# Cross attention and a mixture of experts in one kernel: output projection over pairs of heads, and ten subtractions per batch moved to GpSimd

## The reference

```python
# attention: B=8 batches, N=512 tokens, M=1024 keys, 8 heads of 64, D=256
q, k, v = layernorm(x) @ Wq, context @ Wk, context @ Wv
attn = softmax(q @ k.T * 64 ** -0.5)          # by head
x = x + tanh(g_xattn) * (concat_heads(attn @ v) @ Wo + bo)
# experts: 4096 tokens, 8 experts, the best 2 of each token, capacity 1280
h = layernorm(x)
top2, selected = top_k(softmax(h @ router.T), 2)
y = (pre(h) * silu(gate(h))) @ post           # by expert, DFF=1024
x = x + tanh(g_ffn) * scatter_add(y * weight)
```

## Time and profile before

| | |
|---|---|
| time, median of 3 runs | 1711.11 us (1710.55 to 1712.54) |
| profiled execution, its own time | 1709.52 us |
| its span | 1707.8 us |
| attention, to the first expert matmul | about 1079 us |
| a middle batch, start to start | 131.4 us |
| TensorE, VectorE, ScalarE, GpSimd busy | 96%, 74%, 61%, 39% of the span |

### The profile page before, as it was taken

The page is one execution under the profiler, slowest core; times in us unless marked ns, Lnnn a source line. Parts: engine busy times, 40 slices in busy tenths (PEclk is TensorE's granted clock), DMA queues, the critical chain, the costliest instruction groups (busy, mean ns, idle before and its releaser), DMA issues.

```text
span 1707.8 us, 33525 instructions
## 1 busy us (share of the span) xinstructions
PE 1640.7 (96%) x12454; PEld 1494.2 (87%) x12454; DVE 1262.5 (74%) x2597; ACT 1048.9 (61%) x2179; POOL 672.5 (39%) x629
## 2 busy tenths in 40 slices
PE   6999999999999999999999998989999999999997
PEld 5788888888888888888888886889999999999997
DVE  6888888888888888888888878666565656547443
ACT  5767766666766767667766667536454555546443
POOL 3352444444345345345245334423343422332322
PEclk9999999999999999999999999999999999999999
DMA  4300210111121121031031032314423421341211
GB/s 127 125 26 1 93 71 26 76 75 39 56 96 38 36 106 48 15 124 51 13 125 39 14 137 72 134 42 110 115 39 108 113 37 29 109 115 29 38 33 27
DMA packets 60555, 115.49 MB, mean 68 GB/s; under 512 B 6616, under 2 KB 48480, under 8 KB 59776
## 3 DMA queue, kind: packets, MB, share of 16 engines
q1 hardware_dynamic: 37104, 79.24, 13.1%
q0 software_dynamic: 15392, 18.66, 6.1%
q10 hardware_dynamic: 7920, 15.73, 2.6%
HBM read 90.27 MB, written 57.42 MB: 86 GB/s over the span
## 4 chain that ended last, share of the span: by engine, by line
PE 73%; DVE 13%; issue 5%; POOL 4%; ACT 3%; DMA 2%; POOLq 0%; ACTq 0%; DVEq 0%; SPq 0%; another core or an unknown queue 0%
PE ring L1236 11%; PE turned L1130 10%; PE ffn L1093 10%; PE ffn L1095 10%; PE ffn L1094 10%; PE scores L1118 9%; DVE neg_max L1931 5%; PE ring L1093 3%; PE ring L1095 3%; PE ring L1094 3%; DVE pt_l L1708 3%; PE ring L1202 1%; DMA out<-y,y_token 1%; PE ring L1204 1%; POOL lists L884 1%
## 5 line engine op out<-in xcount | busy, mean ns | idle before, releaser
L918 POOL TENSOR_SCALAR probs<-probs,row_rec 128x1024 f32<-128x1024 f32 x254 | 282.3, 1124 | 465.9 <-DVE row_rec L2035 454.4
L1472 ACT ACTIVATE pt_h<-turned 128x512 fp32r<-128x512 f32 x512 | 278.7, 601 | 208.1 <-PE turned L1130 208.1
L1708 DVE TENSOR_TENSOR pt_l<-turned,pt_h 128x512 fp32r<-128x512 f32 x512 | 331.6, 680 | 6.4 <-ACT pt_h L1472 6.4
L1931 DVE TENSOR_REDUCE neg_max<-scores 128x1 f32<-128x1024 f32 x256 | 302.3, 1217 | 34.7 <-PE scores L1118 34.6
L1130 PE MATMUL turned<-ident,probs 128*128 128x128 f32 x2048 | 281.1, 279 | 27.0 <-DVE pt_l L1708 19.6
L1130 PEld LDWEIGHTS turned<-ident,probs 128*128 128x128 f32 x2048 | 223.9, 141 | 94.9 <-issue 61.6
L1528 ACT ACTIVATE probs<-scores,neg_max 128x1024 f32<-128x1024 f32 x256 | 285.3, 1116 | 13.8 <-DVE neg_max L1931 12.6
L1236 PE MATMUL ring<-pt_h,v_hl 128*128 128x256 f32 x1024 | 261.3, 293 | 0.8
L1236 PE MATMUL ring<-pt_l,v_hl 128*128 128x256 f32 x1024 | 250.7, 283 | 0.0
L2301 DVE TENSOR_TENSOR act_f<-ffn,silu 128x256 f32<-128x256 f32 (+1 forms) x232 | 108.4, 467 | 125.7 <-ACT silu L1642 114.8
L1236 PEld LDWEIGHTS ring<-pt_h,v_hl 128*128 128x128 f32 x1024 | 195.7, 191 | 4.9 <-issue 3.6
(11 more groups left out here) (260 smaller groups left out, 3903.0 us busy)
## 6 DMA issues: line engine op xcount, KB each, us to landing
lists<-pads SPq DMA_DIRECT2D x8, 4160.0 KB
w_raw<-w_t ACTq DMA_DIRECT2D x10, 1024.0 KB, 8.7
e_rows<-lists SPq DMA_DIRECT2D x26, 390.0 KB
ctx_raw<-ctx_t SPq DMA_DIRECT2D x15, 512.0 KB, 3.8
wg_raw<-wg_t ACTq DMA_DIRECT2D x5, 1024.0 KB, 7.7
x_in<-x SPq DMA_DIRECT2D x8, 512.0 KB, 4.1
x_sum<-x SPq DMA_DIRECT2D x8, 512.0 KB, 3.9
out<-x_sum SPq DMA_DIRECT2D x8, 512.0 KB, 2.9
```

Source lines behind the costliest of these rows:

```text
L918: nc.gpsimd.tensor_scalar(probs[:, k, :], probs[:, k, :], row_rec[:, k:k + 1], 1.0, ALU.mult, ALU.mult).then_inc(scaled, 1)
L1472: return nc.scalar.activation(dst, src, ACT.Copy)
L1708: return nc.vector.tensor_tensor(dst, src, hi_part.bitcast(F32), ALU.subtract)
L1931: nc.vector.tensor_reduce(neg_max[:, k:k + 1], scores[:, n % 2, :].rearrange("p (a c) -> p a c", a=2), AX.XY, ALU.max, negate=True).then_i ...
```

## The change

The values of two heads now lie so that one head's own rows are 0 to 63 and the other's 64 to 127: the two heads fill one tile of 128 rows, `ot_h` by pairs. The rows with the product of v's low halves go to `o_low` by ScalarE, VectorE writes `o_rest` (value minus its high half), and GpSimd adds both to `ot_l` (`join_low`, one for two `o` jobs, at each step divisible by 4). A `w` job is two pairs by three passes: 6 matmuls, and it waits for GpSimd's join (`ot_done`). Wo is held once, and is split in one piece. VectorE's subtraction after an `o` job waits for ScalarE's first copy alone; TensorE waits for both copies.

Ten of the 16 k and v jobs of a batch (`POOL_LOWS`) are no longer drained by VectorE: ScalarE copies the bank a second time, raw, into `raw_of_job`, and that releases the bank; GpSimd subtracts later, at the steps of `POOL_LOWS_AT`. The first batch keeps these on VectorE, the last has eight of them.

```diff
@@ FIRST_JOBS
-    15: [("w", 0, 0)],
-    16: [("w", 0, 1), ("k", 3, 0)],
-    17: [("v", 1, 3)],
+    16: [("w", 0, 0), ("k", 3, 0)],
+    17: [("v", 1, 3), ("w", 0, 1)],
     18: [("h", 1, 0)],
-    19: [("w", 0, 2), ("l", 0, 0)],
-    20: [("k", 3, 1), ("q", 3, 0)],
+    19: [("l", 0, 0)],
+    20: [("w", 0, 2), ("k", 3, 1), ("q", 3, 0)],
@@
+POOL_LOWS = [("k", 1, 0), ("k", 1, 1), ("k", 2, 0), ("k", 2, 1), ("v", 1, 0), ("v", 1, 1), ("v", 1, 2),
+             ("v", 1, 3), ("v", 0, 0), ("k", 0, 0)]
+POOL_LOWS_AT = {2: [0], 4: [1], 10: [2], 12: [3, 4], 16: [5, 6], 18: [7], 26: [8, 9]}
@@ gpsimd
+            def join_low(body, u):
+
+                i = ((u - 6) // 4 * 2 + 1) % (2 * H)
+                part, m = i // 4 % 2, i // 2 % 2
+                toks = slice(m * 2 * P, (m + 1) * 2 * P)
+                o = ("o", i, 0)
+                wait_drained(pool, body, body.where[o] if u > 0 else body.before.where[o] - RING)
+                pool.wait_ge(low_copied, at(body.b - 1 if u < 5 else body.b, 2 * H, i + 1))
+                alone(pool)
+                nc.gpsimd.tensor_tensor(ot_l[:, part, toks], o_rest[:, part, toks], o_low[:, part, toks],
+                                        ALU.add).then_inc(ot_done, 1)
+
+            def low_of_job(body, n):
+
+                kind, i, j = POOL_LOWS[n]
+                wait_drained(pool, body, body.where[POOL_LOWS[n]])
+                raw = raw_of_job[:, RAW_SLOT[n], :]
...
+                nc.gpsimd.tensor_tensor(dst, raw, hi_part.bitcast(F32), ALU.subtract)\
+                    .then_inc(lows_split, 1)
@@ gpsimd step, behind the scaling of the probabilities
+                    if u == 0 and body.prev or u % 4 == 0 and body is not END and \
+                            (body.prev if u < 8 else body.own):
+                        join_low(body, u - 2)
+                    if body.prev and body.own:
+                        for n in POOL_LOWS_AT.get(u, ()):
+                            if POOL_LOWS[n] in body.where:
+                                low_of_job(body, n)
@@ tensor
-                    o = ("o", H * i + H // 2 + 1 + j // 2 * 2, 0)
-                    reads = [body.before.where[o] - RING if i == 1 and j < 2 else body.where[o]]
+                    pe.wait_ge(ot_done, at(b - 1 if i == 1 else b, H, 4 * i + 3 + j // 2))
@@
-                    for h in range(H // 2):
-                        head = i * (H // 2) + h
-                        nc.tensor.matmul(bank[:, 0:D], ot_h[:, h, toks], wo_h[:, head, :],
-                                         start=h == 0, stop=False)
-                        last = nc.tensor.matmul(bank[:, 0:D], ot_x[:, h, toks], wo_x[:, head, :],
-                                                start=False, stop=h == H // 2 - 1)
+                    for part in range(2):
+                        pair = 2 * i + part
+                        last = passes(bank[:, 0:D], (ot_h[:, part, toks], ot_l[:, part, toks]),
+                                      (wo_h[:, pair, :], wo_l[:, pair, :]), part == 0, part == 1)
@@ scalar
-                    hi(ot_x[0:DH, h % 4, toks], bank[0:DH, 0:2 * P])
-                    last = hi(ot_h[:, h % 4, toks], bank[:, 0:2 * P])
+                    main, low = slice(ab * DH, (ab + 1) * DH), slice((1 - ab) * DH, (2 - ab) * DH)
+                    hi(ot_h[main, pair % 2, toks], bank[main, 0:2 * P]).then_inc(hi_done[kind], 1)
+                    hi(o_low[main, pair % 2, toks], bank[low, 0:2 * P]).then_inc(low_copied, 1)
+                    return
...
+                if body.lows_on_pool(what):
+                    n = POOL_LOWS.index(what)
+                    until(act, lows_split, at(body.b - 1, len(POOL_LOWS), RAW_FREE[n]))
+                    hi(raw_of_job[:, RAW_SLOT[n], :], bank).then_inc(drained[c % 2], 1)
@@
-                    if body is FIRST and u in (5, 6):
-                        half = u - 5
-                        part = slice(half * 4, half * 4 + 4)
-                        act.wait_ge(raw_loaded[3 + half], 16 * 2)
-                        hi(wo_x[DH:P, part, :], wo_raw(half)[DH:P, :, :])
-                        hi(wo_h[:, part, :], wo_raw(half)).then_inc(raw_hi, 1)
+                    if body is FIRST and u == 5:
+                        act.wait_ge(raw_loaded[3], 16)
+                        hi(wo_h[:, :, :], x_sum[:, :, :]).then_inc(raw_hi, 1)
@@ vector
-                if kind == "h":
+                if kind == "h" or body.lows_on_pool(what):
                     return
@@
-                    last = lo(ot_x[DH:P, h % 4, toks], bank[0:DH, 0:2 * P], ot_h[0:DH, h % 4, toks])
+                    main = slice(ab * DH, (ab + 1) * DH)
+                    last = lo(o_rest[main, pair % 2, toks], bank[main, 0:2 * P], ot_h[main, pair % 2, toks])
```

More of the change, by code:

```diff
@@ L203, in of, with attended_at, lows_on_pool @@
         return Body(b, self.prev, self.own, self.nxt, self.offset, FIRST if b == 1 else self.before)
+    def attended_at(self, c):
+        for job, place in self.where.items():
+            if place == c and job[0] == "o":
+                return (self.b - 1 if self.step_of[job] < 5 else self.b), job[1]
+        for job, place in self.before.where.items() if self.before else ():
+            if place - RING == c and job[0] == "o":
+                return (self.b - 2 if self.before.step_of[job] < 5 else self.b - 1), job[1]
+        return None
+    def lows_on_pool(self, job):
+        return self.prev and self.own and job in POOL_LOWS
     def route_from(self):
@@ L1243, in run_job @@
                 reads = wait_for_job(body, u, what)
-                wait_all_drained(pe, body, reads + [c - 2] +
-                                 [c - 1] * (body is END and what[0] in "hlr"))
+                free = [c - 2] + [c - 1] * (body is END and what[0] in "hlr")
+                wait_all_drained(pe, body, reads + free)
+                for o in [body.attended_at(place) for place in free]:
+                    if o:
+                        pe.wait_ge(low_copied, at(o[0], 2 * H, o[1] + 1))
                 do_job(what, ring[:, bank_of(body, what, c), :])
```

81 lines of the change are left out of this document (46 added, 35 removed).

## The result

The changed kernel takes **1739.36 us** (median of 4 runs, 1739.05 to 1739.59); the kernel before, on the same chip, 1711.05 (4 runs). The ratio is 1.0164, 95% interval 1.0146 to 1.0181: slower, by 28.3 us. The forecast was 1725, its range ended at 1738.

The account below looks back on a forecast made before the run. TensorE was taken as the bound, 96% busy with some waits. Six middle batches at +2.8 (16.8), first batch -4.5, last +2.4 and closing join +0.5 made +15.2 on 1709.5, given as 1725 us; range 1691 to 1738.

Parts of the forecast that it names:

- I take +1.1: Step 16, middle batch: VectorE's small steps wait for GpSimd's join and subtraction, delaying the row maximum; +1.1 us, bounds 0 to 1.3.
- Its four w jobs stand at fuller steps: -1.0: First batch, without moved subtractions: its four shorter w jobs save 1.0 us.
- The Wo part: First batch: Wo split once, so TensorE's waits at 53.52 and 59.54 go; 3.5 us saved with the step before them.
- The closing stage: Behind the last batch: the join stands before the first w job once more, +0.5 us.
- The last batch ahead of it: Last batch, with eight subtractions and without those of steps 24 to 28: +2.4 us.
- Steps 10 and 12, +0.8: Middle batch: step 10's GpSimd subtraction meets L1750, delaying normalisations and the scaling behind; +0.8 us, bounds 0 to 1.3.
- At steps 20 and 22 likewise: none: Middle batch: TensorE's next job waits for a bank there, so shorter w jobs gain nothing.
- step 28 +0.4: Middle batch: the join lies over the small steps making scatter row numbers, moving scatters and step 0; bounds 0 to 0.7 us.
- the w jobs at steps 2 and 18: Middle batch: the chain has 0.6 us of slack there, so two fewer matmuls give -0.24 us each.
- Step 0's wait: Start of a middle batch: w waits 0.8 to 0.85 us for GpSimd's join, less 0.24 for the shorter job: +0.6.
- Step 24's +0.5: Middle batch: the join puts `ctx_l` 0.75 us later, with `pt_l` and transposes following, partly given back; bounds -0.3 to +1.4.
- The rival that TensorE gets its matmuls back: VectorE's lighter queue shortens the chain from scores to `pt_l`, w jobs count in full; about 1693 us, chance 0.2.

Follow-up runs that it names:

- x11_fill_wait: The changed kernel with TensorE making step 16's projection job twice in every middle batch and the last, ahead of its wait; 1731.83 us, ratio 1.0137.
- x3_copy: x4_pairs_only plus a dummy ScalarE copy of 128x512 on a scratch tile behind each of the ten high halves; 1727.71 us.
- x1_busy16: x4_pairs_only plus two dummy GpSimd subtractions of 128x512 at step 16 of every middle batch and the last, which nobody reads; 1719.93 us.
- x8_best: x4_pairs_only with most joins ahead of GpSimd's scaling, step 0's in the batch before, and x7_first_places' first-batch places; 1711.55 us, ratio 1.0019.
- x5_other_steps: The changed kernel with GpSimd's two step 16 subtractions put at step 18 and step 10's at step 12; 1729.12 us.
- x4_pairs_only: The changed kernel with the ten low halves back on VectorE and no raw ScalarE copies; paired projection and joins stay; 1719.89 us, ratio 1.0070.
- x12_no_shift: x4_pairs_only with ScalarE's second copy of attended values not shifted by 64 partitions, so low terms land at wrong heads; 1717.7 us.
- x10_copy_busy16: x4_pairs_only with both x3_copy's dummy ScalarE copies and x1_busy16's dummy GpSimd subtractions at step 16; 1735.78 us.
- x9_lows_best: x8_best with the ten low halves on GpSimd, at the steps of x5_other_steps; 1716.57 us.
- x7_first_places: x4_pairs_only with four first-batch projection jobs at other steps (18, 19 and 22 instead of 16, 17 and 20); 1723.42 us.

## Why the prediction was wrong

The direction and most mechanisms were right; the sum was 14 us short, and the time lay 1.4 us beyond the range. The steps that failed:

- **"I take +1.1" at step 16.** It measured +2.5 as a mean, which is 8.3 us of the miss over six batches. The part that I had argued, VectorE's two small steps stretched by the join and the subtraction behind a later `pt_l`, is +1.3, the upper end of my own bounds, as the one batch without a fall shows. The rest is the granted clock behind the wait, in five batches of six, which I had nowhere. x11_fill_wait prices it at 7.3 us. This is half of the miss. I had the later `pt_l` only as a detail. It is the condition of the rest: in x3_copy ScalarE's copy costs 0.4 us by itself and 0.3 through the join that the small step then meets, and without it GpSimd's subtractions cost nothing (x1_busy16).
- **"Its four w jobs stand at fuller steps: -1.0" in the first batch.** The first batch as a whole gained 0.2 instead of 4.5. The Wo part was right: the steps behind it got 1.33 and 2.18 us shorter, 3.5 together. The jobs' new steps cost +3.3: a wait for VectorE's `pt_l` at step 16, one of 0.62 us for a join at step 20. I had looked at how full these steps were for TensorE, not at what VectorE had behind them. x8_best wins 2.3 of it back by other steps. That is 4.3 us of the miss.
- **The closing stage**, +0.5 for one join: the stage got 2.3 us longer (15.65 to 17.99). TensorE waited 1.59 us for the join, since I had let the join run when its input was there, and it stood behind two scalings; the granted clock of the stage was 0.91 instead of 1.00 as well. The last batch ahead of it got 1.5 us longer, not 2.4: its step 16 rose by 0.04 us where I had +1.1. Together this is 0.9 us of the miss.
- **Steps 10 and 12, +0.8**: measured +0.9, nearly right by size and by luck, since the cause was wrong. Of step 12's +0.7, 0.6 is there without any subtraction at step 10 (x5_other_steps): ScalarE's longer pair of copies gives 0.2 (x4_pairs_only), the raw copy 0.4 (x3_copy). Only step 10's own +0.27 is the subtraction.
- **"At steps 20 and 22 likewise: none"**: step 22 has +0.35. ScalarE's two copies and the exponential no longer overlap, which I had costed at nothing. The exponential there begins 0.25 us later, and TensorE waits for what stands behind it (x4_pairs_only); 0.13 of this is the shift (x12_no_shift).

What held: step 28 +0.4 (measured +0.44), the w jobs at steps 2 and 18 (-0.48 forecast, -0.44 measured) and next to nothing at the other steps, the join at 0.75 (0.73 measured), VectorE's waiting for ScalarE, and the experts' stage. Step 0's wait is 0.24 to 0.69 us in the middle batches instead of 0.85, and its +0.6 came out as +0.3. Step 24's +0.5 is right for the join alone (x4_pairs_only), and the moved jobs give 0.35 of it back. These errors cancel by luck: steps 0 and 24 were 0.6 us a batch too high together, step 22 and the w jobs 0.5 too low. The rival that TensorE gets its matmuls back was excluded by the sign: the row maximum at step 16 starts 1.3 us later behind its scores, not closer. One reading was too wide: the prediction counts L1741 (0.86 us) as agreeing with a rule on two inputs in SBUF, but that instruction reads one tile; L1750 (0.32 us) is its row with two.

## What to carry to other kernels

Work moved off a full engine has to be read at each place of the order where a short instruction with a waiter stands behind it: two moved pieces that cost 0 and 1.0 us a batch alone cost 2.4 together, and moving three of ten subtractions by a few steps gave 13 us of the six middle batches back. Where the bound engine already waits for a chain, each tenth added to that chain counted in full here, and a longer wait may also lower the clock of what follows; filling it with repeated work can be faster than leaving it empty. A helper's operation that someone waits for (here the join) goes ahead of what the helper does next, if its input is there first.

## What the runs showed of the hardware

- TensorE's granted clock after a wait, in steps of middle batches: behind waits of 1.65 to 1.68 us it stayed at 1.00 in 12 of 12 (x3_copy, x5_other_steps), behind 2.0 us it fell in 4 of 6 (x10_copy_busy16), behind 2.2 us in 5 of 6 (the changed kernel), behind 1.5 us in none of 6 (x11_fill_wait). At the lower level 128x256 matmuls start 0.21 us apart, at the upper 0.12. Why the batch at 422.5 escaped with the same wait is open. The length of the wait alone doesn't decide: elsewhere in the traces the clock stayed at 1.00 behind a wait of 1.90 us (the kernel before, at 59.54) and fell to 0.50 behind one of 1.66 (x9_lows_best, at 1046.74, in its last batch). Two waits of 0.73 and 1.01 us with four transposes between them were followed by matmuls at the lower level too (x7_first_places; 0.83 in the window).
- A VectorE instruction on 128x4 elements between tiles ends with the GpSimd instruction that it meets (0.47 us in x10_copy_busy16, 0.65 and 0.72 in the changed kernel; with one input alone 0.78 us, a copy in x12_no_shift), and took 0.19 where it began first, by 0.11 us (x1_busy16). GpSimd's own times hardly show it: the subtraction pair took 2.52 us in the changed kernel and the split of the context 2.54.
- ScalarE's copy with a shift by 64 partitions is not overlapped by the exponential behind it: 0.39 us from start to start instead of 0.28, the same instruction otherwise.
